# Where two batches' products stand in the matmul order of a mixer layer

## The reference, cut to what matters

```
hBC = silu(causal_conv(hBC, conv_w, conv_b))            # 4 taps
M   = einsum('bcihn,bcjhn->bcijh', Ch, Bh) * L          # L = exp(segsum(A*dt))
Y_diag = einsum('bcijh,bcjhp->bcihp', M, hc)            # hc = hid * dt
y   = Y_diag + Y_off + D * hid
yg  = y * silu(gate);  yg *= rsqrt(mean over its group of yg*yg + eps)
out = residual + (yg * gnorm_w) @ out_proj_w.T
```

## Time and profile before

| | |
|---|---|
| time, median of 3 | 2677.43 us |
| span of the profiled execution | 2670.2 us |
| TensorE matmuls busy | 86% of the span |
| VectorE busy | 73% |
| ScalarE busy | 55% |
| GpSimd busy | 46% |

### The profile page before, as it was taken

The page is one execution under the profiler, slowest core; times in us unless marked ns, Lnnn a source line. Parts: engine busy times, 40 slices in busy tenths (PEclk is TensorE's granted clock), DMA queues, the critical chain, the costliest instruction groups (busy, mean ns, idle before and its releaser), DMA issues. The chain is left out here.

```text
span 2670.2 us, 33973 instructions
## 1 busy us (share of the span) xinstructions
PE 2308.2 (86%) x11172; PEld 1672.4 (63%) x11172; DVE 1957.9 (73%) x3153; ACT 1460.8 (55%) x3092; POOL 1238.2 (46%) x788
## 2 busy tenths in 40 slices
PE   5966676667454999999999999999999999779997
PEld 4532222225434677777777777777777777569996
DVE  4559989994554786686685776775866866688777
ACT  2344444443103796685785866866956857742221
POOL 2119988993101464363462553644643624542212
PEclk9989998998576999999999999999999999899999
DMA  2030030000112232231332322322312312211010
GB/s 80 26 115 13 0 126 0 0 0 32 60 36 74 90 119 66 76 115 52 90 99 57 101 76 71 111 72 74 108 67 77 113 52 88 91 45 37 36 48 32
DMA packets 113218, 175.20 MB, mean 66 GB/s; under 512 B 9696, under 2 KB 77664, under 8 KB 112032
## 3 DMA queue, kind: packets, MB, share of 16 engines
q1 hardware_dynamic: 113056, 173.16, 20.6%
HBM read 166.71 MB, written 6.42 MB: 65 GB/s over the span
## 5 line engine op out<-in xcount | busy, mean ns | idle before, releaser
L78 PE MATMUL mg_pb<-xTh,mg_wh 128*128 128x512 f32 x1152 | 479.2, 416 | 16.9 <-POOL mg_wl L1233 16.9
L1243 POOL TENSOR_TENSOR mg_y<-mg_hT,mg_sg 128x512 f32<-128x512 f32 x128 | 187.7, 1466 | 598.9 <-DVE mg_hT L1479 598.9
L79 PE MATMUL mg_pb<-xTl,mg_wh 128*128 128x512 f32 x1152 | 454.3, 394 | 0.0
L80 PE MATMUL mg_pb<-xTh,mg_wl 128*128 128x512 f32 x1152 | 452.1, 392 | 0.0
L775 PE MATMUL ss_y<-ss_pr,cst 128*128 128x512 f32 x512 | 278.5, 678 | 125.7 <-POOL ss_pr L757 125.4
L1427 DVE SCALAR_TENSOR_TENSOR mg_hT<-mg_pb,mg_cw,mg_hT 128x510 f32<-128x510 f32 (+2 forms) x432 | 318.4, 741 | 31.6 <-ACT mg_hT L1599 22.8
L757 POOL TENSOR_TENSOR ss_pr<-o,ss_bc 128x1024 f32<-128x1024 f32 x128 | 301.9, 2374 | 45.9 <-DVE o L726 26.9
L1454 DVE TENSOR_TENSOR mg_m<-mg_gb,mg_cb 128x384 f32<-128x384 f32 x512 | 265.3, 549 | 71.6 <-ACT mg_gb L1649 68.2
L775 PEld LDWEIGHTS ss_y<-ss_pr,cst 128*128 128x128 f32 x512 | 98.4, 210 | 305.6 <-POOL ss_pr L757 225.8
L657 ACT ACTIVATE ss_da<-dt,ss_na 128x510 f32 (+1 forms) x256 | 165.9, 680 | 208.0 <-DVE o L726 208.0
L78 PEld LDWEIGHTS mg_pb<-xTh,mg_wh 128*128 128x128 f32 x1152 | 217.2, 189 | 76.5 <-issue 19.2
(11 more groups left out here) (289 smaller groups left out, 5217.4 us busy)
## 6 DMA issues: line engine op xcount, KB each, us to landing
mg_abc<-acs_rows SPq DMA_DIRECT2D x256, 256.0 KB, 3.4
mg_ws<-in_w_in SPq DMA_DIRECT2D x72, 512.0 KB, 3.8
ss_bc<-bc_rows SPq DMA_DIRECT2D x16, 1024.0 KB, 6.4
mg_wos<-in_w_out SPq DMA_DIRECT2D x64, 256.0 KB, 3.6
ff_ws<-in_w SPq DMA_DIRECT2D x7, 1024.0 KB, 4.7
x<-in_x SPq DMA_DIRECT2D x16, 256.0 KB, 4.1
ip_ws<-in_w_in SPq DMA_DIRECT2D x8, 512.0 KB, 3.6
ff_w2s<-in_w SPq DMA_DIRECT2D x7, 512.0 KB, 5.7
```

Source lines behind the costliest of these rows:

```text
L78: pe.matmul(out, lhs[0], rhs[0], start=start, stop=False)
L79: pe.matmul(out, lhs[0], rhs[1], start=False, stop=False)
L80: return pe.matmul(out, lhs[1], rhs[0], start=False, stop=stop)
L1243: pool.tensor_tensor(yb[:, p % RING, t], hT[s % 2][:, t], sg[s % 2][:, t], ALU.mult).then_inc(s_y2, 1)
```

## The change

TensorE's order in the steps that finish a pair is changed; no instruction is added, removed or altered. In a step with output tiles, batch 0's product moves behind the first output tile and batch 1's moves up beside it, ahead of the third projection. In a step without, batch 0's product moves behind the third projection, beside batch 1's.

```diff
                         proj(s, 1, 0)
                         proj(s, 1, 1)
-                        y_mm(p, 0)
                         if outs:
                             out_tile(*outs[0])
+                            y_mm(p, 0)
+                            y_mm(p, 1)
                         proj(s, 2, 0)
                         proj(s, 2, 1)
-                        y_mm(p, 1)
+                        if not outs:
+                            y_mm(p, 0)
+                            y_mm(p, 1)
                         proj(s, 3, 0)
                         proj(s, 3, 1)
```

## The result

The changed kernel is slower by a little: 2679.4 us median of 22 runs against 2674.2 of 22 runs of the kernel before, ratio 1.0022 with a 95% interval of 1.0014 to 1.0030, that is +3.7 to +8.0 us. The forecast was 2688 us, from +10.8 on 2677.4. The span of the profiled execution went from 2670.2 to 2677.2.

A forecast was written before the change was run, and what follows sets the result against it. TensorE sets the mixer's pace, but VectorE and ScalarE's loop binds r = 8; moved products lengthen steps without tiles. Groups 1 to 7 +9.6, last r = 0 -0.5, group 0 +1.7: +10.8 on 2677.4, 2688 us, range 2680 to 2698.

The forecast's parts named there:

- What bounds the steps: In r = 5, batch 0's later product delays VectorE's kernels 4 to 7 and TensorE's last product: 16.07 against 15.58 us.
- Rival 1: All 64 product visits: VectorE's order is loose enough, each saving counts; -22 us, 2655; chance 0.10 in either form.
- half form: Only the 21 tile steps gain 0.35 us each and the others break even: 7 us, 2670; chance 0.10 in either form.
- The price of going in and out: TensorE's product visits: two apart cost 2.00 us, two together 1.65, so 0.35 saved per step, bounds 0.30 and 0.40.
- r = 6 to 8 and r = 2: r = 6 and 7 together +0.86 us, r = 8 unchanged; r = 2 +0.20 as its first output tile waits for `low`.
- The meeting with GpSimd: In r = 6 and 7 VectorE's differences are held up by GpSimd's work as in r = 8: 16.30 us each.
- r = 0: Groups' step before the next projections: product 2.78 us later, kernel 7 ends at 15.75, 16.63 against 16.11 us, +0.52.
- Rival 3: New waits before last products lower TensorE's clock in all 32 steps r = 5 to 8: +34 us, 2722; chance 0.03.
- 1.05 lost: Price of one clock fall on TensorE after a pause: 15 matmuls took 4.50 us and not 15 x 0.23.
- r = 3 and 4 pause for GpSimd anyway and I take +0.3: Group 0's steps r = 3 and 4: the existing pauses stay, the change adds +0.3 us, within group 0's +1.7.
- The base: Time of the kernel before: profiled span 2670.2 us plus 7.2 for the median of the runs, 2677.4.

The follow-up runs named there:

- e9: Kernel before; in steps without output tiles batch 0's product behind the third projection, batch 1's half a projection later, no visit saved: 2685.3 us, ratio 1.0053.
- e3: Changed kernel with six kernel buffers in place of four and the square's temporary in the gate's buffer: 2664.7 us, ratio 0.9970 against the kernel before.
- e2: Kernel before with the change only in the 21 steps with output tiles: 2668.9 us, ratio 0.9982.
- e4: Kernel before, old order, with six kernel buffers in place of four and the square's temporary in the gate's buffer: 2674.1 us, ratio 1.0002.
- e10: Kernel before with four buffers; products together only in r = 3 and 4 with tiles and group 0's r = 2 and 3: 2662.8 us, ratio 0.9966.

## Why the prediction missed

- **What bounds the steps: right.** The loop "batch 0's product, kernel 4, kernel 7, last product" gave 16.07 for r = 5 and 16.05 came; kernel 4 was forecast at 10.27 into the step and started at 10.24 (1504.40 - 1494.16). e9 and e3 show both halves: late without the saving is as long, and without the wait the saving is there.
- **Rival 1, every saved visit counts: wrong**, for the reason given against it. Of its half form only r = 3 and 4 hold, which gain 0.40 each (forecast 0.35, bounds 0.30 and 0.40); r = 2 loses, and the other steps don't break even. In e3's r = 5 a visit less was worth 0.46. The price of going in and out was put 0.05 to 0.1 us too low.
- **r = 6 to 8 and r = 2: right** within 0.14 us for the three together and 0.04. The meeting with GpSimd is there as forecast: in r = 6 of the changed kernel kernel 4 starts 10.24 into the step, and the first difference takes 0.58 us and ends 0.08 behind GpSimd's square sum. r = 0 was put 0.17 too low, and its cause is open. For all that follows group 0 this leaves +10.5 against +9.1.
- **Rival 3, the clock: wrong.** TensorE's waits of up to 1.0 us for kernels left it at 1.00 in groups 1 to 7, ahead of the mixer's last step, and so did 0.77 us in group 0. Its price was also too low: "1.05 lost" counted 15 matmuls of 0.23 us in the stretch, but three of the 15 are transposes, and the same work at full clock shows 1.56 lost. That a pause of 2.36 us had left the clock at 1.00 could be read from the trace of before, one step after the earlier trace rows.
- **The step that failed** is in the sum: "r = 3 and 4 pause for GpSimd anyway and I take +0.3". They gave -4.9: the pauses shrank by 4.35 us, the clock that no longer fell gave 1.56, and the change's own price was 1.0. The pause was taken as fixed, since its end hangs on GpSimd. But which GpSimd instruction the fourth difference meets hangs on 0.47 us that the change itself moves. The rows for a closer look were there: in the earlier trace rows VectorE and GpSimd are both busy 5.94 of 6.10 us while TensorE stands. I gave group 0 no bound below zero and no rival.
- **The base** was too high as well. The run of the changed kernel that was profiled took 2679.1 for a span of 2677.2, 1.9 over it. The 7.2 that I put over before's span compared one execution's span with the median of others. From 22 runs before stands at 2674.2, so 3.2 us of the miss are the base. The change itself was put at 10.8, and the mixer says 7.0: 5.2 too much in group 0 and 1.4 too little behind it. The medians say 5.2; the 1.8 between the two is within what executions differ by.

Left open: before's runs spread from 2660.5 to 2677.6. Group 0's pauses are not the same in each trace of the old order (r = 4 took 18.1 in before's and e2's and 20.0 in e4's), and the part ahead of the mixer varies; how much of the spread each makes was not measured.

## What to carry to other kernels

Moving a small piece of work later on the busiest engine gains its switching cost only where nobody waits for its result; count the row of work behind the first reader up to the point where the busiest engine needs it back, and change those steps alone in which that sum leaves room. Here 14 steps picked so and two of the first group gained 9 us (e10), and the change in all steps cost 5. And treat a pause that another engine's long instruction causes as a matter of phase: ask which instruction is met, and by how much the change shifts the two against each other.

## What the hardware showed that was not expected

- A shift of 0.47 us decided whether TensorE paused 2.71 or 0.77 us: a 128x128 TENSOR_SCALAR on VectorE took 0.28 us alone, 0.44 to 1.10 beside GpSimd's shorter instructions and 2.37 beside a 2.39 us one, and single ones passed in a gap of 0.1 us between GpSimd's.
- The granted clock in the 4.5 us after a pause, ahead of the mixer's last step: 1.00 behind pauses of up to 1.07 us and, twice, behind one of 2.36 (before, e2); 0.62 each of the four times behind one of 2.67 to 2.71 (before, e2, e4 twice). The fall cost 1.56 us, 13.88 against 12.32 (before; 13.88 in e4's r = 4 too). What lies between 2.36 and 2.67, and whether the length of the pause alone decides it, no run shows.
- One visit less of the 64-wide products between 128x512 matmuls was worth 0.40 us in each of 14 tile steps, 0.46 in r = 5 with six buffers, and 0.39 in TensorE's wait.
